# One float32 product per time step of a recurrence, issued as four products of 32 columns

## The reference

```python
xW = jnp.einsum('ntd,dh->nth', x, Wx) + b
xW_t = jnp.swapaxes(xW, 0, 1)
def step(prev_h, xw):
    next_h = jnp.tanh(prev_h @ Wh + xw)
    return (next_h, next_h)
_, h_t = jax.lax.scan(step, h0, xW_t)
```

## Time and profile before

| | us |
|---|---|
| median of three runs | 229.57 |
| the profiled execution's own time | 229.55 |
| its span, first to last instruction | 227.8 |
| PE busy, of the span | 223.4 (98%) |
| DVE busy | 138.7 (61%) |
| ACT busy | 108.2 (48%) |

### The profile page before, as it was taken

How to read it: one execution, slowest core, us unless ns; L and a number is a source line. 1 busy time by engine, 2 the same in 40 slices (tenths; PEclk the granted TensorE clock), 3 DMA queues, 4 the chain that set the end, 5 groups by cost and what they waited for, 6 DMA issues and landing times.

```text
span 227.8 us, 8577 instructions
## 1 busy us (share of the span) xinstructions
PE 223.4 (98%) x3465; PEld 208.2 (91%) x3465; DVE 138.7 (61%) x786; ACT 108.2 (48%) x773; POOL 0.5 (0%) x5
## 2 busy tenths in 40 slices
PE   7999999999999999999999999999999999999995
PEld 7899999999999999999999999999999999999984
DVE  3656666666666666666666666666666666666653
ACT  1344544455444554445544455444554445544452
POOL 0000000000000000000000000000000000000000
PEclk9999999999999999999999999999999999999999
DMA  6799930202020020202002020100202011020211
GB/s 190 219 398 415 406 140 12 86 0 98 3 92 3 3 92 4 96 3 92 3 3 94 4 95 0 77 21 4 94 3 95 0 53 45 4 94 3 95 46 49
DMA packets 6717, 18.41 MB, mean 81 GB/s; under 512 B 1171, under 2 KB 2454, under 8 KB 6678
## 3 DMA queue, kind: packets, MB, share of 16 engines
q1 hardware_dynamic: 6528, 17.71, 20.4%
q10 hardware_dynamic: 150, 0.15, 0.2%
HBM read 9.48 MB, written 8.39 MB: 78 GB/s over the span
## 4 chain that ended last, share of the span: by engine, by line
PE 97%; ACT 1%; DVE 0%; issue 0%; ACTq 0%; DVEq 0%
PE banks L241 58%; PE banks L232 33%; PE banks L221 3%; PE banks L207 2%; PE banks L215 1%; ACT L178 1%; ACT tanh_z L178 0%; ACT z L180 0%; DVE h_t L334 0%; DVE silu L359 0%; ACT h_t L198 0%; DVE ones L338 0%; DVEq L401 0%; ACTq L197 0%; ACTq L177 0%
## 5 line engine op out<-in xcount | busy, mean ns | idle before, releaser
L241 PE MATMUL banks<-h,wh_a 128*128 128x32 f16 x1530 | 132.8, 179 | 0.0
L392 DVE TENSOR_TENSOR h<-h_t,h 128x32 f16<-128x32 f32 x510 | 74.7, 188 | 81.0 <-ACT h_t L198 81.0
L232 PE MATMUL banks<-x,wx_sb 128*128 128x128 f32 x512 | 113.0, 305 | 0.0
L241 PE MATMUL banks<-h_t,wh_last 128*128 128x32 f32 x510 | 104.1, 286 | 0.0
L241 PE MATMUL banks<-h,wh_b 128*128 128x32 f16 x765 | 102.7, 176 | 0.0
L195 ACT ACTIVATE h<-banks 128x32 f16<-128x32 f32 x255 | 50.3, 197 | 110.1 <-PE banks L241 108.5
L241 PEld LDWEIGHTS banks<-h,wh_a 128*128 128x128 f16 x1530 | 86.1, 96 | 14.3
L232 PEld LDWEIGHTS banks<-x,wx_sb 128*128 128x128 f32 x512 | 75.9, 189 | 0.2 <-issue 0.2
L241 PEld LDWEIGHTS banks<-h_t,wh_last 128*128 128x128 f32 x510 | 75.8, 188 | 0.0
L241 PEld LDWEIGHTS banks<-h,wh_b 128*128 128x128 f16 x765 | 62.8, 97 | 0.0
L198 ACT ACTIVATE h_t<-banks 128x64 f32<-128x64 f32 x256 | 57.1, 223 | 0.8 <-PE banks L241 0.6
(11 more groups left out here) (33 smaller groups left out, 11.8 us busy)
## 6 DMA issues: line engine op xcount, KB each, us to landing
x<-in_x SPq DMA_DIRECT2D x15, 512.0 KB, 10.9
out_dram<-h_t SPq DMA_DIRECT2D x15, 512.0 KB, 2.6
x<-in_x SPq DMA_DIRECT2D x2, 256.0 KB, 5.0
wh_floor<-in_wh SPq DMA_DIRECT2D x1, 256.0 KB, 2.9
w_t<-in_w SPq DMA_DIRECT2D x1, 256.0 KB, 4.1
wx_sb<-in_wx SPq DMA_DIRECT2D x1, 256.0 KB, 4.9
out_dram<-h_t SPq DMA_DIRECT2D x1, 256.0 KB, 2.1
w_t<-in_w_cond SPq DMA_DIRECT2D x1, 145.0 KB, 2.6
```

Of the source, the lines that this page charges most:

```text
L232: return nc.tensor.matmul(pre[c % 2][e][m][:, steps, :], wx_sb[:, k, m * P:(m + 1) * P], moving, start=False, stop=False, skip_group_check ...
L241: return nc.tensor.matmul(pre[t // CS % 2][s % 2][m][:, s // 2, :], weights, h_part, start=start, stop=stop, skip_group_check=True)
L392: nc.vector.tensor_tensor(h2[:, t % 2, m, :], h_t[:, c, m, cols], h1[:, t % 2, m, :], ALU.subtract).then_inc(h2_ready[m], 1)
```

## The change

In the step, the call at line 305 is replaced by a call of a new function, `recur_last`, which issues four products in place of one. Product q takes columns q to q+31 of `wh_last` as weights, all 128 partitions of the same moving operand, and writes partitions q to q+31 of the same piece of PSUM. In the built program each of the four has a tile of 128 rows by 32 columns of PE's array, at column 0, 32, 64 or 96. Every other product keeps the tile of 128 by 128. The wait for `h_ready` stands on the first of the four; there is no wait on the other three, and the values summed are the same. No instruction of another engine changes or moves, and no instruction of PE changes its place relative to the rest.

```diff
+            def recur_last(t, h_part):
+                s = t % CS
+                for q in range(0, P, 32):
+                    nc.tensor.matmul(pre[t // CS % 2][s % 2][0][q:q + 32, s // 2, :], wh_last[:, q:q + 32], h_part,
+                                     start=False, stop=False, skip_group_check=True)
...
                     pe.wait_ge(h_ready, t)
-                    recur(t, 0, wh_last[:], h_last)
+                    recur_last(t, h_last)
                     pe.wait_ge(h2_ready[0], t)
```

## The result

The changed kernel takes 239.59 us (median of 4 runs, 239.26 to 239.86) against 229.57 before: a ratio of 1.041, 95% interval 1.037 to 1.046. It is slower, as forecast, but by 10.0 us and not by 35.7. That lies inside the band of the forecast's own case (237 to 285 us), but at its lower edge and far from its point, 265 us.

What follows compares the result with a forecast made beforehand. The loop was line 198, DVE, line 307 and the products behind it. Shape changes of 0.07 and 0.08 less 0.01 us slack gave 0.14 us per step, 255 x 0.14 = 35.7 us on 229.55: 265 us, range 229 to 302.

Steps and rivals of the forecast that it cites:

- the forecast's own case: Partial wait at each change of array shape around the four products: 0.03 to 0.22 us per step, 237 to 285 us; chance 0.38.
- stated most of 2.6: Removing line 305's float32 product gains 0, at most 0.01 us per step, 2.6 us in all.
- rival 4: Float32 product, not DVE, holds line 307; four tiles side by side take 0.054 us: 41 us gained, 188 us; chance 0.05.
- The two gaps at the switches: Sign in the profile after: gaps before and behind the four tile products together near 0.15 us over the usual.
- The switch in: From line 303's last float16 matmul to the first tile load: 0.07 us late, between bounds of 0 and 0.14.
- The switch out: From the last tile matmul to line 307's load: 0.08 us, between bounds of nothing and another 0.15.
- the cost of the four products: At line 305, eight load and matmul pairs of 32 columns take 0.20 to 0.22 us, taken as 0.216.
- the budget: 0.22 us that DVE's first subtraction leaves the float32 product before line 307's load, from 102.05 to 102.27.

Runs made afterwards that it cites:

- the float32 kernel on the whole array: Against the kernel before: no float16 split or DVE subtraction, all four blocks of Wh as float32 products on the whole array; 544.6 and 558.7 us.
- the three kernels with the most of them: 32-column tiles: changed kernel with every loop product tiled, 416.3 us; kernel without float16 split with recurrent products tiled, 284.4 us, or input and bias too, 329.9 us.

## Why the prediction was wrong

**Where it held.** The float32 product had next to nothing to give: leaving it out brought 1.4 us, inside the stated most of 2.6, and rival 4's gain of 41 us is out. The two gaps at the switches are together 0.17 us over the usual, close to the 0.15 that the forecast gave as a sign. The switch in was put at 0.07 us and measured 0.07. The switch out was put at 0.08 over the usual and measured 0.10 (0.124 less 0.025), since the float32 tile matmul has a record of 0.196 where 0.176 had been taken. The mechanism, an array that must be empty while 0.07 us of fetching overlaps, fits four records of different length (0.176, 0.196, 0.223 and 0.275 us), each with 0.07 left at its end. What PE does in these 0.07 us no run shows. The page's rule (the Trainium skill, TensorEngine Tiling (Array Packing), Key Properties) that a new tiling mode drains TensorE agrees with the trace: the load of the new shape stands 0.104 and 0.124 us behind the last matmul's start, where 0.00 to 0.03 was seen between products of one shape with no wait between them. Neither the clock nor, but for one pause of 0.4 us, the supply of instructions moved in the change.

**The step that failed** is the cost of the four products: "Eight pairs are 0.20 to 0.22 us, and I take 0.216". The bounds from both sides, 0.025 and 0.054 us per pair, were both for pairs that follow one another. Measured, the last matmul starts 0.074 us behind the first load: loads and matmuls of different tiles start 0.007 us apart, and only the two loads of one tile wait for each other (0.028 us apart with one tile alone, 0.055 with 64 columns). From the first tile load to where an ordinary next load could start it is 0.074 + 0.025 = 0.10 us and not 0.216. This term was 0.116 us too long, and the switch out 0.02 too short; part of one error hid in the other. Together they are 0.10 us per step, 255 times that is 25 us, and 265 less 25 is 240, where 239.6 was measured.

The rule that points to this was in hand: the Trainium skill (TensorE: Matmul & The Clock Gate, Measured speedup vs the span model) puts products in different column groups some 4 ns apart. The trace agrees in kind, with 6 to 7 ns. In the prediction it was used only for a rival in which the product held the line. It was not carried into the forecast's own case, where a short product pays for much of the two switches. With the 0.054 us that rival 4 gave to four tiles side by side, the forecast's own sum is 0.07 + 0.054 + 0.08 = 0.20 us, which lies under DVE's 0.22, and the time would not have changed. With the 0.10 us that was measured, it is 0.25, which is 0.03 us per step over, some 237 us. A lower bound taken from a whole-array row was no bound on tiles.

**A smaller misreading** is the budget. "The two paths are level to within 0.01 us, and DVE's is the last" was read from the loads. At the matmul of line 307 PE came last, by 0.016 us. That did little to the sum: the load of line 307 comes 0.267 - 0.226 = 0.041 us later than before. From that load to line 313's matmul it is now 0.118 us in place of 0.125, since the matmul no longer stands 0.02 behind its load. That leaves 0.034, and the step grew by 0.037 (medians, good to some 0.002). 255 times 0.037 is 9.4 us. The other 0.4 us of the spans' 9.8 is the pause of PE that the groups put down to issue.

## What to carry to other kernels

Find out first whether the operation to be shortened holds anything: here a group that kept a 98% busy engine busy for 104 us was worth 1.4 us, and the experiment that leaves it out says so, if it leaves no second wait behind. Look at the start of the matmul too, and not only at that of its load, to see who holds a line. When products in another tile shape stand between whole ones, charge each change of shape with the last matmul's record less 0.07 us, and the tiles themselves with little (0.05 us for one, 0.07 for four); switch where PE waits anyway, or not at all. Count the instructions too: where the program had one load or matmul for less than some 16 ns of its time, PE ran dry.

## What the runs showed that was not expected

- Two waits on one PE instruction put its load 0.12 us behind the releasing engine, where one wait gives 0.05 (248.7 against 228.15 us, with a fall of the granted clock to 0.85 on top). Why the second wait costs this was not taken apart.
- Taking work off PE can cost more than the work: that kernel, without the product but with both waits, was 19 us slower than with it. And a PE that is under way in 99% of the span can be held at the lower of its two clock levels from 16 us to the end (the float32 kernel on the whole array, mean 0.51).
- PE's loads and matmuls came no faster than one per 15 to 16 ns over whole programs, in the three kernels with the most of them. That the fetch of 16 KB blocks sets this is an inference from the queue's counts and the idle time put down to issue; no run changed the fetch alone.
